# Expert layer on one core: the weight split behind the last activation, a drain replaced by a count, weight sums spread over seven experts

## The chip, the cores and the metric

The kernel runs on one core of one Trainium2 chip. The metric is the device time of one execution, in microseconds; lower is better. Engine names in the profile: PE is TensorE (PEld its weight loads), DVE is VectorE, ACT is ScalarE, POOL is GpSimd, SP is SyncE, which only issues DMAs here.

## What is computed

Four residual layers over 4096 tokens of width 256: a linear-memory attention, a mixture of experts, an RWKV time and channel mix, and a gated network with ternary weights. The change lies in the mixture of experts, and in the preparation of sums of the last layer's hidden weights, which runs beside it. The mixture, as the reference has it (top 2 of 8 experts, hidden size 1024):

```
logits = xf @ w_router
probs = softmax(logits); topk_w, topk_idx = top_k(probs, 2)
h = gelu(einsum('te,ieh->tih', xf, w1) + b1)
out = einsum('tih,ihe->tie', h, w2) + b2
out = sum(out * weights[..., None], axis=1)
```

## The kernel before

**Tiles.** The stage before has sorted the tokens by expert, as rows `z1_by_expert` in memory. A tile is 256 rows of one expert; there are 35 tiles here, four or five per expert, and their number per expert is read at run time. Each engine runs `expert_tiles`: for every expert one call of its `step` for the first tile, and a loop of `step` for the others. In the first tile `before` is the expert before, in the others it is the expert itself; the test `before < e` so marks an expert's first tile.

**Products.** Every matrix product is made of three, from a high and a low part of each operand (`mm3`, lines 1468 to 1470). The parts: high = a copy rounded to the short form, low = raw minus high. For weights, ScalarE makes the high part (`high_part`, line 1654) and VectorE the low part (`low_part`, line 1740), each 128 x 2048 elements; both matrices of an expert have two buffers, used in turn. For the hidden activations `h`, VectorE makes both parts, two blocks of 128 at a time (lines 1757 and 1759).

**One tile on TensorE** (`step` of `pe`): `up(e, t)`, 8 blocks m of 6 matmuls, into four banks used in turn; from block 4 on a block waits until ScalarE has taken the one four blocks before (`h_act`, the GELU of line 1665). Then `rows_T(t + 1)`, four transposes of the next tile's rows, and `down(before, t)`, 48 matmuls on the h of the tile before. `hs_free` tells VectorE after each quarter of `down` that a pair of h has been read. After `down` in an expert's first tile TensorE drains and increments `ex_done` (line 1629).

**One tile on ScalarE**: in a first tile, if there is a next expert (`ahead`: experts 0 to 6), wait until its weights have landed and make the high part of its w1; 8 GELUs; in a first tile wait for `ex_done` and make the high part of w2; then `gated(t)` (line 1651): wait for both halves of `yt` and for the landing of the scatter before (`y_out`), and scale by the gates into `yg`.

**One tile on VectorE**: gates; in a first tile the low part of the next w1; `rows_split(t + 1)` (the next tile's rows, lines 1713 to 1717); four pairs of h, of which the fourth comes behind `y(before, t)`, the bias sums `yt` (line 1725), one for each of the two banks of `down`; the rows' token numbers (line 1730), `hand_on` (line 1735); in a first tile the low part of the next w2.

**One tile on POOL**: two scatters with addition of `yg` to the token rows (line 1542, `y_out`). In the first tile of experts 1 to 6 `hidden_sums` is called behind it (lines 1547 to 1561): DMAs that add one 512 x 512 block of a hidden weight matrix in memory to another, in halves of 512 KB, all in POOL's queue like the scatters. Experts 1 and 2 have four of them, 3 to 6 two. In expert 7 two multiplications for the next stage's weights follow (line 1534). SyncE loads the rows of tiles ahead, and the raw weights of expert e + 2, two buffers in turn.

Of the kernel before, what the change touches and what calls it, by code (L numbers as in the profile page):

```python
# [28 lines left out]
NP7 = 7  # L29
# [47 lines left out]
def build(nc, A):  # L77
# [5 lines left out]
    with ctx:  # L83
# [1369 lines left out]

        ew_rdy, ex_done = sem2("w1_split"), sem2("expert_done")
        eb_ld, xg_ld, xt_ps, xT_rdy = (sem2("expert_biases_loaded"), sem2("rows_loaded"), sem2("rows_T_in_psum"),
# [70 lines left out]
        def _(pool):  # L1526
# [17 lines left out]

            def add_blocks(to, source):
                for k in (0, 2):
                    pool.dma_start(hw_rows[to][:, k:k + 2, :], source[:, k:k + 2, :], accum_op=ALU.add).then_inc(hw_add, 16)

            def hidden_sums(n):

                layer, base = n % 2, n % 2 * NP7
                if n < 2:
                    pool.wait_ge(hw_cp, 16 * 2 * NP7)
                    for i in (W_S3, W_S1):
                        add_blocks(base + i, quarter(layer, 1, 0))
                elif n < 4:
                    pool.wait_ge(hw_add, 16 * 8)
                    add_blocks(base + W_S2, hw_rows[base + W_S1])
                elif n < 6:
                    pool.wait_ge(hw_add, 16 * 12)  # L1560
                    add_blocks(base + W_S4, hw_rows[base + W_S2])

# [18 lines left out]
        def _(pe):  # L1581
            T = nc.tensor
            pe.sem_inc(xt_ps, 1)
            pe.sem_inc(ex_done, 2)

# [36 lines left out]
            def step(e, t, before, start):  # L1622

                up(e, t)
                rows_T(t + 1)
                if not start:
                    down(before, t)
                    if before < e:
                        pe.drain().then_inc(ex_done, 1)

# [6 lines left out]
        def _(act):  # L1637
# [18 lines left out]
            def step(e, t, before, start):  # L1656
                ahead = before < e and e + 1 < NE
                if ahead:
                    act.wait_ge(*landed(e + 1))
                    high_part(w1s, raw1, e + 1)  # L1660
                for m in range(KH):
                    act.wait_ge(up_ps, t * KH + (m + 1))
                    if m % 2 == 0:
                        act.wait_ge(h_rdy, t * 4 + (m // 2 + 1))
                    nc.scalar.activation(h32[:, m, :], B[m % 4][:, 0:TT], ACT.Gelu_apprx_tanh,  # L1665
                                         bias=b1s[:, e * KH + m:e * KH + m + 1]).then_inc(h_act, 1)
                    if start and m == 5:
                        act.wait_ge(ew_rdy, 1)
                        act.wait_ge(w2_rdy, 1)
                        act.dma_start(st1[:, :, :], w1_d[2]).then_inc(nw_ld[0], 16)  # L1670
                        act.dma_start(st2[:, :, :], w2_d[2]).then_inc(nw_ld[0], 16)
                if ahead:
                    act.wait_ge(ex_done, e + 2)
                    high_part(w2s, raw2, e + 1)
                if not start:
                    gated(t)
# [10 lines left out]
        def _(dve):  # L1687
# [54 lines left out]
            def step(e, t, before, start):  # L1742
                ahead = before < e and e + 1 < NE
                gate_of(e, t)
                if ahead:
                    low_part(w1s, raw1, e + 1, 2 * e + 3, ew_rdy)
                rows_split(t + 1)
                for m in range(0, KH, 2):
                    i = m // 2
                    dve.wait_ge(h_act, t * KH + (m + 2 + 4))  # L1750
                    if i < 3:
                        dve.wait_ge(hs_free, t * 3 + (i + 1))
                    else:
                        if not start:
                            y(before, t)
                        dve.wait_ge(dn_ps, t * 2 + 2)
# [1678 lines left out]
```

## Time and profile before

| | us |
|---|---|
| three timed runs | 2024.34, 2028.38, 2029.12 |
| their median | 2028.38 |
| the profiled execution | 2018.43 |
| its span | 2016.4 |
| expert stage in it (first transposes to last product) | about 522 to 962 |
| TensorE busy over the span | 1829.2 (91%) |
| VectorE busy | 1488.2 (74%) |
| ScalarE busy | 1114.2 (55%) |
| GpSimd busy | 316.7 (16%) |

Busy time is how long an engine executed; the rest is idle. In a timeline a bracket behind an instruction gives how long its engine had been idle before it and whose work ended that. Matmuls are pipelined: each is drawn 0.28 us long while the next begins 0.11 us after it.

### The profile page before, as it was taken

The page shows a single profiled execution, that of the slowest core. Times are in us where ns is not written, and L with a number is a line of the kernel's source. Part 1 is how long each engine was busy: PE and PEld are TensorE (multiplying, and loading weights), DVE is VectorE, ACT ScalarE, POOL GpSimd, SP SyncE. Part 2 cuts the span into 40 slices and gives each one's busy share as a digit, 9 for nine tenths or more (in the row PEclk, how much of TensorE's full clock was granted, in tenths as well). Part 3 has the DMA queues.
Part 4 walks back from the last instruction along what each step waited for, and adds up shares of the span by engine and source line. Part 5 has one row for each costly group of instructions (what it writes and reads, how often), then busy time and mean ns, then how long its engine had stood idle before and what let it go on. Part 6 is the DMA issues. An engine that isn't in the chain of part 4 may idle for free. (4 is left out here: it accounts for less than half of the span.)

```text
span 2016.4 us, 31206 instructions
## 1 busy us (share of the span) xinstructions
PE 1829.2 (91%) x10840; PEld 1561.6 (77%) x10840; DVE 1488.2 (74%) x2966; ACT 1114.2 (55%) x1987; POOL 316.7 (16%) x282
## 2 busy tenths in 40 slices
PE   8999999996598899999577758999999999999999
PEld 5688888885598899999455536677788888888887
DVE  7567888787566666666599879999686776776675
ACT  4656666663444344343688857665456456456454
POOL 0000012234344233333100011111000000000000
PEclk9999999995799999999788879999999999999999
DMA  3199434413456545442444553333333143143141
GB/s 110 50 389 402 127 123 143 146 65 121 121 115 141 116 89 109 70 64 38 125 112 88 111 100 132 150 124 123 122 142 146 34 176 146 41 177 117 53 177 64
DMA packets 107986, 251.79 MB, mean 125 GB/s; under 512 B 8992, under 2 KB 51616, under 8 KB 99616
## 3 DMA queue, kind: packets, MB, share of 16 engines
q1 hardware_dynamic: 82288, 201.16, 28.2%
q0 software_dynamic: 23680, 46.28, 12.4%
q10 hardware_dynamic: 1888, 2.67, 0.4%
q8 instruction: 75, 1.23, 0.3%
q14 instruction: 55, 0.45, 0.1%
HBM read 172.88 MB, written 107.61 MB: 139 GB/s over the span
## 5 line engine op out<-in xcount | busy, mean ns | idle before, releaser
L1542 POOL DMA_INDIRECT tokens_behind_spare_rows<-yg,row_of_token x70 | 128.9, 1841 | 295.6 <-DVE row_of_token L1730 265.3
L1665 ACT ACTIVATE h<-bank,b1s 128x256 f32<-128x256 f32 x280 | 124.0, 471 | 33.5 <-PE bank L1470 21.1
L3172 ACT ACTIVATE hidden_quarter<-hidden_quarter,scl 128x512 f32<-128x512 f32 x96 | 67.6, 721 | 118.9 <-DVE hidden_quarter L3008 117.8
L1651 ACT ACTIVATE yg<-yt,own_gates 128x256 f32<-128x256 f32 x68 | 30.8, 501 | 183.3 <-DVE yt L1725 162.2
L1223 PE MATMUL bank<-st,L 128*128 128x128 f32 x768 | 117.4, 279 | 13.3 <-DVE st L573 13.2
L957 ACT ACTIVATE L<-bank 128x512 f32<-128x512 f32 x128 | 75.1, 593 | 94.7 <-PE bank L1215 94.4
L2381 PE MATMUL bank<-split_0h,hidden_weights 128*128 128x512 f32 x320 | 126.5, 395 | 0.0
L2381 PE MATMUL bank<-split_1h,hidden_weights 128*128 128x512 f32 x320 | 125.4, 392 | 0.1
L2382 PE MATMUL bank<-split_0l,hidden_weights 128*128 128x512 f32 x320 | 125.3, 391 | 0.0
L2382 PE MATMUL bank<-split_1l,hidden_weights 128*128 128x512 f32 x320 | 125.3, 391 | 0.0
L1215 PE MATMUL bank<-L 128*128 128x128 f32 x640 | 119.4, 277 | 0.0
L1223 PEld LDWEIGHTS bank<-st,L 128*128 128x128 f32 x768 | 100.6, 193 | 17.8 <-DVE st L573 7.0
L573 DVE TENSOR_TENSOR st<-st,bank 128x256 f32<-128x256 f32 x192 | 75.1, 417 | 52.9 <-PE bank L1223 52.1
L1214 PE MATMUL bank<-L 128*128 128x128 f32 x512 | 101.4, 280 | 0.7
L2381 PE MATMUL bank<-split_2h,hidden_weights 128*128 128x512 f32 x256 | 101.4, 396 | 0.0
L1759 DVE TENSOR_TENSOR hsl<-h,hsh 128x512 fp32r<-128x512 f32 x140 | 96.9, 692 | 4.8
L2382 PE MATMUL bank<-split_2l,hidden_weights 128*128 128x512 f32 x256 | 100.2, 391 | 0.0
L1215 PEld LDWEIGHTS bank<-L 128*128 128x128 f32 x640 | 95.5, 194 | 0.0
L1468 PE MATMUL bank<-xTh,w_1h 128*128 128x256 f32 x288 | 80.8, 281 | 11.0 <-ACT h L1665 8.9
L1468 PE MATMUL bank<-xTh,w_0h 128*128 128x256 f32 x272 | 78.3, 288 | 12.7 <-ACT h L1665 9.5
L2960 DVE SCALAR_TENSOR_TENSOR hidden_quarter<-bank,scl,x_tok 128x512 f32<-128x512 f32 x64 | 47.4, 748 | 55.6 <-ACT x_tok L3135 55.6
L2967 DVE TENSOR_TENSOR split_2l<-hidden_quarter,split_2h 128x1024 fp32r<-128x1024 f32 x48 | 59.1, 1253 | 35.4 <-ACT split_2h L3154 35.4
(485 smaller groups left out, 6020.2 us busy)
## 6 DMA issues: line engine op xcount, KB each, us to landing
hidden_weights<-hidden_weight_blocks SPq DMA_DIRECT2D x64, 1024.0 KB, 4.9
z_by_expert<-zero SPq DMA_DIRECT2D x64, 520.0 KB, 15.7
hidden_weight_blocks<-in_ffn_dram SPq DMA_DIRECT2D x14, 1024.0 KB, 9.8
ckb<-in_ffn_dram POOLq DMA_DIRECT2D x32, 352.0 KB, 5.5
xg<-z_by_expert SPq DMA_DIRECT2D x36, 260.0 KB, 3.3
x_tok<-in_w_dram SPq DMA_DIRECT2D x8, 1024.0 KB, 10.1
x_tok<-x_T SPq DMA_DIRECT2D x16, 512.0 KB, 6.3
x_tok<-after_time_mix SPq DMA_DIRECT2D x15, 512.0 KB, 8.5
```

Of the source, the lines that this page charges most:

```text
L573: V.tensor_tensor(z_ if SQUARES <= n < LEVELS - 1 else x_, x_, B[2 + j][:, 0:256], ALU.subtract if n == 0 else ALU.add).then_inc(ap_rdy, 1)
L957: A_.activation(L[:, p, j, (n + 1) % 2, :, :], src, ACT.Copy).then_inc(sq_cp, 1)
L1214: T.matmul(B[j][:, 256 * m:256 * m + 128], b_, a, start=True, stop=True)
L1215: last = T.matmul(B[j][:, 256 * m + 128:256 * m + 256], a, b_, start=True, stop=True)
L1223: last = T.matmul(B[2 + j][:, 0:256].rearrange("p (a m d) -> p a m d", a=2, m=2)[:, :, m, :], Ln[:, 2 * m + 1, :], right, start=True, stop ...
L1468: nc.tensor.matmul(out, a[0], b[0], start=first, stop=False)
L1542: pool.indirect_dma_start(x2_d, bass.IndirectOffsetOnAxis(to_row[:, j:j + 1].bitcast(u32), 0), yg[:, j, :], None, compute_op=ALU.add).then ...
L1665: nc.scalar.activation(h32[:, m, :], B[m % 4][:, 0:TT], ACT.Gelu_apprx_tanh, bias=b1s[:, e * KH + m:e * KH + m + 1]).then_inc(h_act, 1)
L1759: V.tensor_tensor(hs[1][:, m:m + 2, :], h32[:, m:m + 2, :], f32(hs[0][:, m:m + 2, :]), ALU.subtract).then_inc(h_rdy, 1)
L2381: nc.tensor.matmul(out, w, x[0], start=first, stop=False, **more)
L2382: return nc.tensor.matmul(out, w, x[1], start=False, stop=last, **more)
L3172: A_.activation(QB[to][:, m, :], src, ACT.Gelu, scale=scl[:, off[lay.name] + row:off[lay.name] + row + 1]).then_inc(g_act, 1)
```

## The change

Three edits. ScalarE's high part of the next w1 moves from ahead of the eight GELUs to behind them, and VectorE's low part of it from ahead of the row split to ahead of `y`, behind the third pair of h. The drain of TensorE and its semaphore `ex_done` go; ScalarE waits for `dn_ps`, which the last matmuls of `down` increment and which VectorE's `y` waits for already. The 16 adding DMAs are issued at experts 1 to 7 as 2, 2, 2, 2, 2, 3, 3, in place of 4, 4, 2, 2, 2, 2, with the waits for the sums that they read.

```diff
--- before.py
+++ after.py
@@ -1451,7 +1451,7 @@
             second_sems.append(ptwo.enter_context(nc.semaphore(name)))
             return second_sems[-1]
 
-        ew_rdy, ex_done = sem2("w1_split"), sem2("expert_done")
+        ew_rdy = sem2("w1_split")
         eb_ld, xg_ld, xt_ps, xT_rdy = (sem2("expert_biases_loaded"), sem2("rows_loaded"), sem2("rows_T_in_psum"),
                                        sem2("rows_T_split"))
         up_ps, h_act, h_rdy, dn_ps, y_rdy, y_out = (sem2("up_in_psum"), sem2("gelu_done"), sem2("h_split"),
@@ -1542,23 +1542,30 @@
                     pool.indirect_dma_start(x2_d, bass.IndirectOffsetOnAxis(to_row[:, j:j + 1].bitcast(u32), 0), yg[:, j, :], None,
                                             compute_op=ALU.add).then_inc(y_out, 16)
 
-            def add_blocks(to, source):
-                for k in (0, 2):
-                    pool.dma_start(hw_rows[to][:, k:k + 2, :], source[:, k:k + 2, :], accum_op=ALU.add).then_inc(hw_add, 16)
-
             def hidden_sums(n):
 
-                layer, base = n % 2, n % 2 * NP7
-                if n < 2:
+                def add(layer, to, half, more=None):
+                    base = layer * NP7
+                    source = quarter(layer, 1, 0) if more is None else hw_rows[base + more]
+                    k = 2 * half
+                    pool.dma_start(hw_rows[base + to][:, k:k + 2, :], source[:, k:k + 2, :], accum_op=ALU.add).then_inc(hw_add, 16)
+
+                if n == 0:
                     pool.wait_ge(hw_cp, 16 * 2 * NP7)
-                    for i in (W_S3, W_S1):
-                        add_blocks(base + i, quarter(layer, 1, 0))
-                elif n < 4:
-                    pool.wait_ge(hw_add, 16 * 8)
-                    add_blocks(base + W_S2, hw_rows[base + W_S1])
-                elif n < 6:
-                    pool.wait_ge(hw_add, 16 * 12)
-                    add_blocks(base + W_S4, hw_rows[base + W_S2])
+                for half in range(2):
+                    if n < 4:
+                        add(n % 2, (W_S3, W_S1)[n // 2], half)
+                    elif n < 6:
+                        pool.wait_ge(hw_add, 16 * 8)
+                        add(n % 2, W_S2, half, W_S1)
+                if n == 5:
+                    pool.wait_ge(hw_add, 16 * 10)
+                    add(0, W_S4, 0, W_S2)
+                if n == 6:
+                    pool.wait_ge(hw_add, 16 * 13)
+                    add(0, W_S4, 1, W_S2)
+                    for half in range(2):
+                        add(1, W_S4, half, W_S2)
 
             def step(e, t, before, start):
                 add_to_tokens(t)
@@ -1581,7 +1588,6 @@
         def _(pe):
             T = nc.tensor
             pe.sem_inc(xt_ps, 1)
-            pe.sem_inc(ex_done, 2)
 
             def rows_T(n):
 
@@ -1625,8 +1631,6 @@
                 rows_T(t + 1)
                 if not start:
                     down(before, t)
-                    if before < e:
-                        pe.drain().then_inc(ex_done, 1)
 
             pe.sem_inc(hs_free, 3)
             rows_T(0)
@@ -1655,9 +1659,6 @@
 
             def step(e, t, before, start):
                 ahead = before < e and e + 1 < NE
-                if ahead:
-                    act.wait_ge(*landed(e + 1))
-                    high_part(w1s, raw1, e + 1)
                 for m in range(KH):
                     act.wait_ge(up_ps, t * KH + (m + 1))
                     if m % 2 == 0:
@@ -1670,7 +1671,9 @@
                         act.dma_start(st1[:, :, :], w1_d[2]).then_inc(nw_ld[0], 16)
                         act.dma_start(st2[:, :, :], w2_d[2]).then_inc(nw_ld[0], 16)
                 if ahead:
-                    act.wait_ge(ex_done, e + 2)
+                    act.wait_ge(*landed(e + 1))
+                    high_part(w1s, raw1, e + 1)
+                    act.wait_ge(dn_ps, t * 2 + 2)
                     high_part(w2s, raw2, e + 1)
                 if not start:
                     gated(t)
@@ -1742,8 +1745,6 @@
             def step(e, t, before, start):
                 ahead = before < e and e + 1 < NE
                 gate_of(e, t)
-                if ahead:
-                    low_part(w1s, raw1, e + 1, 2 * e + 3, ew_rdy)
                 rows_split(t + 1)
                 for m in range(0, KH, 2):
                     i = m // 2
@@ -1751,6 +1752,8 @@
                     if i < 3:
                         dve.wait_ge(hs_free, t * 3 + (i + 1))
                     else:
+                        if ahead:
+                            low_part(w1s, raw1, e + 1, 2 * e + 3, ew_rdy)
                         if not start:
                             y(before, t)
                         dve.wait_ge(dn_ps, t * 2 + 2)
```

## Rows read from the trace of the kernel before

**Rows 1.** the page: busy time of TensorE, its granted clock in 40 slices

```profile
PE 1829.2 (91%) x10840; PEld 1561.6 (77%) x10840; DVE 1488.2 (74%) x2966; ACT 1114.2 (55%) x1987; POOL 316.7 (16%) x282
...
PEclk9999999995799999999788879999999999999999
```

**Rows 2.** the windows: us, busy us of each engine, PEclk, DMA share, GB/s

```profile
750.00:810.00 60.00, 58.00 (x500) 57.61 (x499) 40.19 (x92) 25.60 (x52) 20.49 (x12) 1.00 0.48 97
```

**Rows 3.** the waits of TensorE, 500 to 975: total us, times, longest

```profile
PE bank L1468 <- ACT h L1665: 18.4, 10, 3.7
```

**Rows 4.** the timeline: start, length, what, idle before; first tile, expert 3

```profile
681.26 0.39 PE L1468 MATMUL bank<-xTh,w_1h 128*128 128x256 f32 x1 [1.45 <-ACT h L1665]
```

**Rows 5.** timelines at the end of that tile; groups L1740 and L1629

```profile
689.46 0.69 DVE L1759 TENSOR_TENSOR hsl<-h,hsh 128x512 fp32r<-128x512 f32 x1
690.07 0.77 DVE L1725 TENSOR_TENSOR yt<-bank,b2s 128x256 f32<-128x256 f32 x2
...
L1740 DVE TENSOR_TENSOR w_1l<-x_tok,w_1h x8: 2283/2288/2293, 527.3 to 874.3; 128x2048 fp32r<-128x2048 f32 x8
...
690.46 1.92 ACT L1654 ACTIVATE w_0h<-st 128x2048 fp32r<-128x2048 f32 x1 [5.66 <-PEq L1629]
692.28 0.89 ACT L1651 ACTIVATE yg<-yt,own_gates 128x256 f32<-128x256 f32 x2
693.08 2.71 ACT L1665 ACTIVATE h<-bank,b1s 128x256 f32<-128x256 f32 x6
...
690.89 0.38 PE L1468 MATMUL bank<-xTh,w_1h 128*128 128x256 f32 x1 [0.52 <-issue]
...
L1629 PEldq DRAIN  x7: 2307/2307/2308, 581.4 to 916.0; - x7
```

**Rows 6.** timelines around the sums; DMA issues with landing; windows of the clock

```profile
591.74 5.46 POOL L1547 DMA_DIRECT2D hidden_weight_blocks<-in_ffn_dram  x4
698.46 2.37 POOL L1547 DMA_DIRECT2D hidden_weight_blocks<-hidden_weight_blocks  x2
707.12 1.55 POOL L1542 DMA_INDIRECT tokens_behind_spare_rows<-yg,row_of_token  x1 [0.30 <-issue]
...
tokens_behind_spare_rows<-yg,row_of_token POOLq DMA_INDIRECT x1, 4.1
...
st<-in_w_dram SPq DMA_DIRECT2D x1, 1024.0 KB, 10.2
...
612.59 0.91 ACT L1651 ACTIVATE yg<-yt,own_gates 128x256 f32<-128x256 f32 x2 [10.65 <-DMA tokens_behind_spare_rows<-yg,row_of_token]
...
613.90 0.39 PE L1468 MATMUL bank<-xTh,w_1h 128*128 128x256 f32 x1 [3.66 <-ACT h L1665]
...
666.39 0.38 PE L1468 MATMUL bank<-xTh,w_0h 128*128 128x256 f32 x1 [3.48 <-ACT h L1665]
...
612.00:619.00 7.00, 5.09 (x44) 5.10 (x45) 2.35 (x9) 4.25 (x10) 3.09 (x2) 1.00 1.01 316
...
666.00:672.00 6.00, 5.61 (x35) 5.61 (x36) 1.27 (x7) 3.32 (x8) 3.07 (x2) 0.72 0.63 126
```

**Rows 7.** timelines of expert 7

```profile
908.58 2.09 ACT L1665 ACTIVATE h<-bank,b1s 128x256 f32<-128x256 f32 x5 [0.51 <-DVE hsl L1759]
...
923.61 4.23 POOL L1534 TENSOR_TENSOR x_tok<-x_tok 128x768 f32<-128x768 f32 x2
...
925.20 2.68 DVE L1713 COPY raw_gates<-xg 128x8 f32<-128x8 f32 x1 [4.46 <-PE bank L1591]
...
934.49 0.38 PE L1468 MATMUL bank<-xTh,w_1h 128*128 128x256 f32 x1 [0.94 <-ACT h L1665]
```

**Rows 8.** the timeline of SyncE in the channel-mix stage

```profile
1206.07 1.71 SPq L2439 DMA_DIRECT2D hidden_weights<-hidden_weight_blocks  x3
```

**Rows 9.** timelines of expert 0, second tile

```profile
535.27 0.38 PE L1468 MATMUL bank<-xTh,w_0h 128*128 128x256 f32 x1 [1.66 <-ACT h L1665]
...
536.85 1.40 ACT L1665 ACTIVATE h<-bank,b1s 128x256 f32<-128x256 f32 x3
```


## The prediction

> **What bounds the kernel now.** I read the page first: TensorE is busy 91% of the span, and its clock is at its higher level nearly throughout [rows 1]. Then the stretches of the expert stage, about 520 to 962 us, where all the edits lie: in its steady part TensorE is busy 58 of 60 us, VectorE 40, ScalarE 26 [rows 2]. So only idle time of TensorE can be won there. The list of who waited for whom says what it idles for: ten times for a GELU of ScalarE, 18.4 us in total, the longest 3.7 us [rows 3]. The timelines at an expert's change show where these are.
>
> A tile is 48 matmuls up and 48 down, 0.116 us each start to start (58.0 us by 500 [rows 2]). The up half needs GELU 0 of its own tile before its 25th matmul, 2.8 us after its first. A gap of TensorE listed as idle g costs g + 0.17, since a matmul is drawn 0.28 us long but follows the last after 0.11.
>
> Three kinds of gaps. **First**, in the first tile of experts 1 to 6 ScalarE does the high part of the next w1 (1.92 us) ahead of the GELUs, and TensorE idles 1.45 us [rows 4] (the 1.92 is a row of [rows 5]): loss 1.62, six times: six of the ten waits of [rows 3] are of this kind. **Second**, behind the down half of that tile TensorE drains, and its next up half starts 0.52 us idle later: loss 0.69, seven times [rows 5]. **Third**, in the third tile of experts 1 and 2 ScalarE waits 10.65 us for the scatter of the tile before (it overwrites `yg`), and TensorE idles 3.66 and 3.48 us: loss 3.83 and 3.65. Behind the second the clock is 0.72 of full over 6 us: 0.28 x 6 = 1.7 us more; behind the first it stays at 1.00 [rows 6].
>
> **The change part by part**, on the profiled execution, 2018.43 us with a span of 2016.4.
>
> **(a) High and low part of w1 moved, experts 1 to 6.** The 1.62 of the first kind goes: expert 7, which has no high part, shows its GELUs right behind the gating and no gap [rows 7]. ScalarE then does the high part after GELU 7, in about 5 us in which it waited for the drain (5.66 idle [rows 5]), so that costs nothing. The low part is not so lucky. VectorE has to do it (2.29 us [rows 5]) between the third pair of h and the bias sums `y`. In the timeline the third pair's subtraction starts at 689.46 and ends about 690.15, and `yt` follows at once at 690.07: VectorE has no hole there. So `yt` comes 2.2 us later, at 692.28, done at 693.05; the gating copies of ScalarE wait for both halves of it, run from 693.16, and GELU 0 of the next tile, queued behind them, runs from 693.98 to 694.45 (the spacing 692.28, 693.08 of now). The high part of w2, released by the down products at 690.4, is done at 692.4 and is hidden behind that wait.
>
> **(b) Drain removed.** TensorE's next up half starts at 690.21 in place of 690.89. Its 25th matmul is due 0.68 earlier too, at 692.93, and meets GELU 0 at 694.48: a new loss of 1.55. So for each of experts 1 to 6: -1.62 - 0.69 + 1.55 = -0.76, in all **-4.6**. Even without (a) the drain's gain would mostly be given back: GELU 0 is now ready at 693.55 [rows 5], 0.62 after that earlier due time. Expert 7 has no weights to split, there the whole **-0.7** counts.
>
> **(c) Sums spread.** Now four accumulating transfers are issued in each of the first two places, two in each of four more; after it is two in five places and three in the last two. With four, the second scatter of the next tile lands when it releases ScalarE, at 612.6, that is 20.8 after the first transfer's issue at 591.74; with two it lands 4.1 after 707.12, at 711.2, 12.8 after 698.46 [rows 6]. Without loss ScalarE may get it up to about 17.0 (612.6 - 3.8 - 591.7). So in experts 1 and 2 the wait goes whole: -3.83 - 3.65 - 1.7 = **-9.2**. The bound on the other side: weights of 1 MB from SyncE take 10.2 us in the same stretch [rows 6], and would have to delay the scatter by more than 4 us to bring it back.
> By the Trainium skill (DMA: Bandwidth & Descriptors, Anatomy of one DMA) such a transfer takes 2.0 us plus its bytes over 436 GB/s, 3.2 us for 512 KB. By that four in a row with the two scatters behind them would be through in some 14 us and would delay nobody, and term (c) would be nothing. The rows show 20.8 and the wait; they decide.
>
> Three transfers (experts 6 and 7): between 12.8 and 20.8, at the mean 16.8 against 17.0. No stall, or up to 0.7 each; I take **+0.3**. Nobody is late for the sums: SyncE first reads the blocks at 1206 [rows 8], 260 us behind the last.
>
> **(d) Expert 0.** Here the moved work was free: both parts of w1 of expert 1 ran before or beside the first tile, where everybody waited. After, the high part (1.92) lies ahead of tile 1's GELUs, now at 536.85: GELU 0 ends 539.1 against a 25th matmul due 2.87 after 535.27, 538.1: loss 1.0. The low part delays the splitting of h by 2.2; `yt` of tile 1, by my count of VectorE's queue, comes some 1.1 behind the down products, which costs 0.5 in tile 2. **+1.5**; bounds 1.0 and 2.6 (nothing of the 2.2 absorbed beyond what TensorE already lost) [rows 9].
>
> **(e) Expert 7's products.** POOL's two multiplications for the time-mix weights take 4.23 us from 923.61; VectorE's copy of 128x8 elements, due at 925.20, took 2.68, until they were over, and TensorE lost 0.94 + 0.17 = 1.1 in the next tile [rows 7]. After, three transfers stand ahead of them. Two occupy POOL 2.37, four 5.46 [rows 6], three about 3.5. The products then start near 927, in VectorE's busy part, not with their first 1.6 us in its hole. **+1.6**, between 0 (they interleave as now) and 3.3 (with the clock's 1.7 on a gap that grows to 2.7).
> The Trainium skill (SBUF — State Buffer, two separate sides) says that the port pair of VectorE and GpSimd is an exclusive lock held for a whole instruction by whichever starts first. By that the whole 4.2 us count against VectorE, which gives the same 1.6; the copy's 2.68 agrees. If it did not hold at the new place, the term would be 0.
>
> Sum: -4.6 - 0.7 - 9.2 + 0.3 + 1.5 + 1.6 = **-11.1 us**, 2007.3 on the profiled execution. The median of the three timed runs is 2028.38, 10 above the profiled one and with a spread of 4.8; none of the terms hangs on that, so 2028.4 - 11.1 = **2017.3**.
>
> **The rivals.**
> **R1, the low part is hidden.** If VectorE found room for it (pairs of h taken earlier), the 1.55 would not come, nor expert 0's 0.5: 2017.3 - 9.8 = 2007.5. For it: VectorE is busy for 40 of 60 us only. Against: its holes are not in that place, where `yt` follows the third pair at once [rows 5], and program order puts the low part straight ahead of `yt`.
> **R2, the wait for the scatter stays.** Weight loads or the now later scatters keep ScalarE waiting in experts 1 and 2, or the threes stall as the fours did: up to 9.2 comes back, 2026.5. For it: the two expert changes with the long waits are also those with weight loads. Against: with two transfers no place of four shows a wait.
> **R3, slower: the clock.** Six new gaps of 1.55 us and one or two in experts 0 and 7 come behind another tile's end. If each made the clock fall to its lower level (1.2 of 2.4 GHz) for 6 us, as wide as the window of [rows 6], each would cost 3 us: 7 x 3 = 21, 2038. It decides from 11.1/7 = 1.6 us a place, a fall of 3.2 us. Against: six gaps of 1.45 and one of 3.66 left it at 1.00 [rows 2, 6].
> **R4, the change does nothing that shows**: gains in one place turn up as waits in another, (a) and (b) at zero, (d) and (e) at their upper ends: 2028.4 - 9.2 + 2.6 + 3.3 + 1.4 = 2026.5, like R2.
>
> **How the numbers follow.** Forecast 0.60, R1 0.10, R2 and R4 0.20, R3 0.10. Within the forecast the bounds of (c), (d) and (e) reach from 2015 to 2021, and the median of another set of runs moves by some 3 us either way, as the three here do. The range from R1's edge to R2's: 2009 to 2026. About 0.3% (6 us) is what a measurement tells from no change. Faster by more than that (under 2022.3): the forecast and R1, with a part of each lost to the runs' scatter, and some of R2: 0.72. Within: most of R2 and R4 and a tail of the forecast, 0.21. Slower: 0.07, most of R3.
>
> **What the profile would show.** Right: no gap of TensorE in first tiles; a gap of about 1.4 idle in the second tile of experts 1 to 6, with ScalarE's gating waiting for `yt`, and `yt` directly behind the low part; no wait of `yg` on the scatter in experts 1 and 2; no low clock near 666; a gap over 2 us in expert 7. Wrong: no gap in second tiles (R1), `yg` waiting for DMA (R2), a low clock behind the new gaps (R3). The sum would be wrong if the profiled execution's 10 us under the median stood for gaps that I do not see.

## The result, and the profile after

The changed kernel takes 2017.99 us (median of six runs, 2011.9 to 2019.4), the kernel before 2029.06 on the same chip. The ratio is 0.9941, with a 95% interval of 0.9930 to 0.9951: 11 us, or 0.6%, faster. On another chip the same pair gave 0.9947 (0.9933 to 0.9962). The forecast was 2017.3, 11.1 us faster.

The profiled execution after took 2017.27 us. Its page answers to [rows 1]:

```profile
span 2015.1 us, 31198 instructions
PE 1829.8 (91%) x10840; PEld 1563.2 (78%) x10840; DVE 1489.5 (74%) x2966; ACT 1114.9 (55%) x1987; POOL 307.6 (15%) x282
PEclk9999999996699999999788889999999999999999
```

Its span is only 1.3 us below the 2016.4 of the trace before. That looks like no gain at all; why it is one, and where the 11 us are, is told below with the kernel before run again. First the views of the expert stage. The waits of TensorE, which answer to [rows 3] (columns: total us, times, longest):

```profile
PE bank L1468 <- ACT h L1666: 11.8, 8, 3.2
```

Eight waits for a GELU are left of ten, 11.8 us of 18.4. Six of them are one new gap. The timelines of VectorE, ScalarE and TensorE at the end of expert 3's first tile, which answer to [rows 5]:

```profile
687.53 2.29 DVE L1743 TENSOR_TENSOR w_0l<-st,w_0h 128x2048 fp32r<-128x2048 f32 x1
689.73 0.75 DVE L1728 TENSOR_TENSOR yt<-bank,b2s 128x256 f32<-128x256 f32 x2
...
687.87 1.93 ACT L1658 ACTIVATE w_0h<-st 128x2048 fp32r<-128x2048 f32 x1 [3.81 <-PE bank L1470]
690.60 0.91 ACT L1655 ACTIVATE yg<-yt,own_gates 128x256 f32<-128x256 f32 x2 [0.80 <-DVE yt L1728]
691.41 1.55 ACT L1666 ACTIVATE h<-bank,b1s 128x256 f32<-128x256 f32 x4
...
691.92 0.39 PE L1468 MATMUL bank<-xTh,w_1h 128*128 128x256 f32 x1 [1.35 <-ACT h L1666]
```

The low part of w1 runs from 687.53, right where `yt` stood before; `yt` follows at 689.73, 2.2 us later. ScalarE has the high part of w2 done at 689.80 and idles 0.80 us for `yt`, gates, and its GELU at 691.41 releases TensorE's 25th matmul at 691.92, after 1.35 us idle, a loss of 1.51. The gap ahead of it in the first tile [rows 4] and the one behind the drain are gone.

The second place is expert 7, where POOL, VectorE, ScalarE and TensorE answer to [rows 7]; the last line is a window with its clock (columns as in [rows 2]):

```profile
919.94 3.18 POOL L1551 DMA_DIRECT2D hidden_weight_blocks<-hidden_weight_blocks  x3
921.63 5.18 POOL L1534 TENSOR_TENSOR x_tok<-x_tok 128x768 f32<-128x768 f32 x2
...
920.55 0.87 DVE L1716 COPY raw_gates<-xg 128x8 f32<-128x8 f32 x1 [3.48 <-PE bank L1597]
...
922.65 4.45 DVE L1760 CAST hsh<-h 128x512 fp32r<-128x512 f32 x1
...
930.74 0.91 ACT L1655 ACTIVATE yg<-yt,own_gates 128x256 f32<-128x256 f32 x2 [10.15 <-DVE yt L1728]
...
932.06 0.58 PE L1468 MATMUL bank<-xTh,w_1h 128*128 128x256 f32 x1 [3.16 <-ACT h L1666]
...
931.00:938.00 7.00, 5.94 (x28) 5.94 (x29) 1.45 (x6) 3.94 (x10) 3.21 (x2) 0.51 0.91 155
```

The three sums are issued first, and beside them VectorE's copy of 128x8 elements takes 0.87 us in place of 0.17. POOL's products reach into VectorE's busy part, and the copy of the first pair of h, 128x512, takes 4.45 us in place of 0.42. `yt` and the gating come late, TensorE idles 3.16 us, and for the 7 us behind that its clock is 0.51 of full.

The third is the scatter. The waits of ScalarE in the stage:

```profile
ACT yg L1655 <- DVE yt L1728: 177.2, 33, 10.1
ACT yg L1655 <- DMA tokens_behind_spare_rows<-yg,row_of_token: 6.8, 1, 6.8
```

Before, `yg` waited for the DMA twice, 21.1 us in total, one of them the 10.65 of [rows 6]; now it waits once, in expert 6, for 6.8 us. In other tiles it waits 6.2 us there for `yt` anyway, and TensorE shows no gap.

### The profile page after: what moved, and what is told of

Read it like the earlier page. It is cut to its first block and busy times, and to the rows that moved or that the text cites. A ratio compares the mean times of both kernels' runs of the same rounds, so it can differ in the third digit from the quotient of the medians.

```text
span 2015.1 us, 31198 instructions
## 1 busy us (share of the span) xinstructions
PE 1829.8 (91%) x10840; PEld 1563.2 (78%) x10840; DVE 1489.5 (74%) x2966; ACT 1114.9 (55%) x1987; POOL 307.6 (15%) x282
## 3 DMA queue, kind: packets, MB, share of 16 engines
q8 instruction: 75, 1.23, 0.3%
## 5 line engine op out<-in xcount | busy, mean ns | idle before, releaser
L1542 POOL DMA_INDIRECT tokens_behind_spare_rows<-yg,row_of_token x70 | 119.2, 1702 | 298.7 <-DVE row_of_token L1733 277.0
L1666 ACT ACTIVATE h<-bank,b1s 128x256 f32<-128x256 f32 x280 | 123.7, 472 | 36.3 <-PE bank L1470 21.1
L1223 PE MATMUL bank<-st,L 128*128 128x128 f32 x768 | 117.2, 279 | 13.3 <-DVE st L573 13.2
```

Of the source, the lines that this page charges most:

```text
L1223: last = T.matmul(B[2 + j][:, 0:256].rearrange("p (a m d) -> p a m d", a=2, m=2)[:, :, m, :], Ln[:, 2 * m + 1, :], right, start=True, stop ...
L1542: pool.indirect_dma_start(x2_d, bass.IndirectOffsetOnAxis(to_row[:, j:j + 1].bitcast(u32), 0), yg[:, j, :], None, compute_op=ALU.add).then ...
```

## The experiments

Each ratio is of runs against runs of the kernel before on the same chip. "Stage" is what I read from each trace beside it: from the start of the experts' first up product to the start of their last down product. It leaves out what happens ahead of the stage, which differs between executions.

| kernel | median us | before, same chip | ratio (95%) | stage in its trace |
|---|---|---|---|---|
| before, first trace | | | | 436.7 |
| before again | 2027.95 | 2027.18 | 1.0002 (0.9990 to 1.0013) | 439.5 |
| changed | 2017.99 | 2029.06 | 0.9941 (0.9930 to 0.9951) | 429.1 |
| changed again | 2015.91 | 2027.18 | 0.9947 (0.9933 to 0.9962) | 426.3 |
| sums only | 2013.10 | 2018.97 | 0.9964 (0.9951 to 0.9977) | 431.4 |
| sums only, again | 2023.62 | 2031.38 | 0.9962 (0.9951 to 0.9973) | 430.5 |
| w1's parts only | 2017.83 | 2018.97 | 0.9989 (0.9973 to 1.0004) | 435.8 |
| drain only | 2023.10 | 2018.97 | 1.0014 (1.0000 to 1.0028) | 436.4 |
| changed, low part behind yt | 2002.62 | 2018.97 | 0.9915 (0.9894 to 0.9936) | 422.0 |
| the same again | 2015.01 | 2031.38 | 0.9917 (0.9901 to 0.9933) | 421.2 |
| changed, products first | 2013.20 | 2027.18 | 0.9937 (0.9921 to 0.9952) | 424.2 |
| changed, drain back | 2019.27 | 2031.38 | 0.9939 (0.9924 to 0.9955) | 428.4 |
| all three repairs | 2007.80 | 2027.18 | 0.9909 (0.9893 to 0.9925) | 418.9 |
| repairs and POOL's order | 2011.72 | 2031.38 | 0.9901 (0.9884 to 0.9918) | 420.3 |

### The kernel before and the changed kernel, once more

No edit in either.

> The kernel before against itself: ratio 1 within its interval. Its trace tells whether the low clock comes behind one or both waits for the scatter (one in the first trace: 3.4 us of low clock, 1.7 us of loss each).

> The changed kernel once more, against the kernel before on the same chip as the next three. Theory: of the 11 us measured first, the expert stage's own traces hold 7.7 (from its first up product to its last product); the rest is the runs' scatter and the low clock that comes or stays away behind a gap. Expected 7 to 11 us faster. Rival (something outside the stage got faster too): 11 us or more again, and the trace shows it behind the last product of the experts.

The kernel before gave 1.0002 against itself, and a span of 2028.7 us, 12.3 more than its first trace. The difference lies ahead of the experts' products. ScalarE begins the stage by clearing 67 semaphores (line 1640) before it makes expert 0's high parts. The group of these clears (duration in ns as min/median/max, then start of first and last) and the first high part behind them, first trace:

```profile
L1640 ACTq EVENT_SEMAPHORE_RANGE_CLEAR  x67: 41/41/46, 505.2 to 509.5; - x67
...
509.63 3.71 ACT L1643 ACTIVATE w_0h<-st 128x2048 fp32r<-128x2048 f32 x2 [9.99 <-issue]
```

and again, with the first up product of TensorE:

```profile
L1640 ACTq EVENT_SEMAPHORE_RANGE_CLEAR  x67: 1/41/710, 512.1 to 528.4; - x67
...
528.51 1.91 ACT L1643 ACTIVATE w_0h<-st 128x2048 fp32r<-128x2048 f32 x1 [21.68 <-issue]
...
534.37 0.57 PE L1468 MATMUL bank<-xTh,w_0h 128*128 128x256 f32 x1 [3.20 <-DVE xTl L1717]
```

In the one they run from 505.2 to 509.5, in the other from 512.1 to 528.4, single ones up to 0.7 us. The first up product comes 9.6 us later (534.37, against 524.82 in the first trace); with the 2.8 by which the stage itself was longer that makes the 12.3. Of the 9.6, 6.9 were there before the clears began; where they arise I did not follow. The changed kernel's trace is of the second kind (511.1 to 526.7), the kernel before's first trace of the first kind; its first up product comes 7.8 us later (532.66), and so the two spans differ by 1.3 us only. By the stage alone they differ by 436.7 - 429.1 = 7.6, and the two later ones, both of the second kind, by 439.5 - 426.3 = 13.2. The changed kernel timed 10.7 us below on that chip (0.9947), inside the 7 to 11 expected. The rival there, a gain behind the experts, is out: from the end of the last down product to the end of the span it is 1054.6 us in both traces of before, 1053.1 and 1055.4 in those of the changed kernel.

Why 13.2 and not 7.6: in the kernel before again, ScalarE's waits for the scatter, and two windows with the clock (a window's line ends with TensorE's clock, the DMAs' share and GB/s):

```profile
ACT yg L1651 <- DMA tokens_behind_spare_rows<-yg,row_of_token: 22.1, 2, 11.6
...
620.00:632.00 12.00, 7.37 (x51) 7.28 (x51) 2.99 (x10) 4.26 (x10) 3.09 (x2) 0.86 0.84 255
676.00:686.00 10.00, 7.31 (x49) 7.31 (x50) 2.88 (x10) 4.26 (x10) 3.07 (x2) 0.83 0.66 174
```

The clock fell behind both waits, 0.86 over 12 us and 0.83 over 10: 1.7 us of loss each, where the first trace had it behind the second wait alone. The one wait was longer, too (TensorE lost 4.8 at it, not 3.8). The changed kernel's two traces differ as well: behind the gap in expert 7 the low clock lasted 6.8 us in the first and 3.4 in the second, and the stage began at the low clock for 6.0 us in the first and 2.9 in the second (5.4 and 4.9 in those of before).

### The sums alone

```diff
-                if n < 2:
+                if n == 0:
...
-                    for i in (W_S3, W_S1):
-                        add_blocks(base + i, quarter(layer, 1, 0))
+                    if n < 4:
+                        add(n % 2, (W_S3, W_S1)[n // 2], half)
```

(the whole third edit of the change, and none of the others)

> The kernel before with the spread sums alone; w1's parts and the drain stay where they were. Theory: the two waits for the scatter in experts 1 and 2 go (3.83 + 3.65 us) and with them the low clock behind the second (1.7 us), 9.2 in all; in expert 7 three transfers stand ahead of POOL's products, which costs there 2.2 us of gap and, as in the changed kernel's trace, up to 3.4 us of low clock behind it. So 3.6 to 7.0 us faster than before. Rival R2 (the waits for the scatter come back with the weight loads): 0 to 2 us slower, and the trace shows yg waiting for the DMA in third tiles. Rival (most of the measured 11 us comes from the sums): 9 us or more faster.

> The kernel before with the spread sums alone, once more, beside the others of this call. Expected as the first run had it: 5 to 8 us faster than before; rival: on a chip where the low clock comes behind both waits for the scatter, 2 us more.

Measured: 7.3 us faster, and again 7.7 (0.9962 of 2031.38). The first is 0.3 above the band of the first expectation, the second inside its own. TensorE's waits for GELUs, and VectorE's small copy in expert 7:

```profile
PE bank L1468 <- ACT h L1672: 10.8, 7, 2.2
...
915.49 5.50 DVE L1720 COPY raw_gates<-xg 128x8 f32<-128x8 f32 x1 [4.27 <-PE bank L1598]
```

Both long waits are gone. The copy of 128x8 elements, 2.68 us in [rows 7], takes 5.50: three transfers and then the products stand in POOL. It ends with the products, which are drawn from 915.78 to 920.96. The load of the next rows, issued at 921.22 behind the sums, took 10.6 us where the median of the trace is 3.3, and TensorE idled 1.28 us for it. So this kernel holds the change's part (c) and its cost (e) together. The stage is 5.3 us shorter than the first one of before, and in the second pair of traces, where before lost 1.7 more to the clock and 1.0 more to the wait, 9.0. R2 is out: no wait for the scatter came back with the weights' loads.

### w1's parts alone

```diff
-                if ahead:
-                    act.wait_ge(*landed(e + 1))
-                    high_part(w1s, raw1, e + 1)
                 for m in range(KH):
...
                 if ahead:
+                    act.wait_ge(*landed(e + 1))
+                    high_part(w1s, raw1, e + 1)
                     act.wait_ge(ex_done, e + 2)
...
-                if ahead:
-                    low_part(w1s, raw1, e + 1, 2 * e + 3, ew_rdy)
                 rows_split(t + 1)
...
+                        if ahead:
+                            low_part(w1s, raw1, e + 1, 2 * e + 3, ew_rdy)
                         if not start:
                             y(before, t)
```

> The kernel before with the two parts of the next w1 moved, and nothing else: the drain, its semaphore and the sums as before. Theory: 1.62 us are won in the first tile of experts 1 to 6; the low part delays yt by 2.2, GELU 0 of the second tile is ready at about 694.5 on the timeline of expert 3 against a due time of 693.7 behind the drain, a loss of 0.8; net -0.8 six times, +1.4 in expert 0: 3.5 us faster. Rival R1 (the low part is hidden): 9.7 - 1.0 = 8.7 us faster and no gap in second tiles. Rival (the high part's place never mattered): no change.

Measured 2.2 us faster, between 5.4 faster and 0.8 slower, so no change is not excluded by the times. The trace is clearer. TensorE's waits (GELUs, and those behind the drain, called issue):

```profile
PE bank L1468 <- ACT h L1662: 13.8, 10, 4.3
PE bank L1468 <- issue: 3.7, 7, 0.5
```

The six gaps of 1.6 are gone from the first tiles, and in six second tiles there is one of 0.7 (the 0.8 expected) behind the drain's 0.7. Expert 0 lost 1.67. The two scatter waits grew a little (3.71 and 4.46 lost), and the clock fell behind both. R1, the low part hidden, would have been 8.7 us and is refuted.

### The drain alone, and the change with the drain put back

```diff
-                    if before < e:
-                        pe.drain().then_inc(ex_done, 1)
...
-                    act.wait_ge(ex_done, e + 2)
+                    act.wait_ge(dn_ps, t * 2 + 2)
                     high_part(w2s, raw2, e + 1)
```

(and the reverse of it on the changed kernel)

> The kernel before with the drain replaced by the count of down products, nothing else. Theory: TensorE starts the next up half 0.68 us earlier but meets GELU 0 at its 25th matmul 0.62 later than that earlier due time, because ScalarE's high part of w2 takes 1.92 us from the same moment as before: net -0.07 six times and -0.7 in expert 7, so 1.1 us faster, not to be told from no change, and a gap of about 0.45 us idle in second tiles in place of the one behind the drain. Rival (the drain costs what it shows): 0.69 x 7 = 4.8 us faster and no gap in second tiles.

> The changed kernel with the drain and its semaphore back, the other two parts as changed. Theory: yt, late by the low part, sets GELU 0 of the second tile anyway, so experts 1 to 6 lose nothing by the drain (it hides under the 1.5 us gap) and only expert 7 loses 0.7: 0 to 1.5 us slower than the changed kernel, 10 to 11 faster than before. Rival (each drain costs its 0.7): 4.8 us slower than the changed kernel, 6 to 7 faster than before.

The drain alone: ratio 1.0014, from no change to 0.3% slower; a gain of 4.8 us is excluded. ScalarE and TensorE at expert 3's second tile:

```profile
688.50 1.93 ACT L1651 ACTIVATE w_0h<-st 128x2048 fp32r<-128x2048 f32 x1 [5.62 <-PE bank L1470]
690.33 0.89 ACT L1648 ACTIVATE yg<-yt,own_gates 128x256 f32<-128x256 f32 x2
691.12 1.18 ACT L1662 ACTIVATE h<-bank,b1s 128x256 f32<-128x256 f32 x3
...
691.63 0.38 PE L1468 MATMUL bank<-xTh,w_1h 128*128 128x256 f32 x1 [0.44 <-ACT h L1662]
```

The drain's 0.52 idle of [rows 5] has become 0.44 idle at the 25th matmul, because the high part of w2, 1.93 us from the moment that the down products end, sets GELU 0. The changed kernel with the drain back is as fast as without (0.9939 beside 0.9941 and 0.9947), 12.4 us faster than before where 10 to 11 were expected; the rival's 6 to 7 lies outside its interval (9.1 to 15.4). Its timeline of TensorE shows how the 1.5 us splits in two:

```profile
689.90 0.38 PE L1468 MATMUL bank<-xTh,w_1h 128*128 128x256 f32 x1 [0.52 <-issue]
693.46 0.39 PE L1468 MATMUL bank<-xTh,w_1h 128*128 128x256 f32 x1 [0.55 <-ACT h L1669]
```

0.52 behind the drain and 0.55 at the 25th matmul: losses of 0.69 and 0.72, together 1.41 against 1.51. So a wait removed ahead of a later one that it hid under is worth nothing.

In expert 7 the drain's 0.69 was not won either. VectorE and TensorE there, in the drain-only trace:

```profile
922.11 3.67 DVE L1710 COPY raw_gates<-xg 128x8 f32<-128x8 f32 x1 [3.48 <-PE bank L1590]
...
932.39 0.38 PE L1468 MATMUL bank<-xTh,w_1h 128*128 128x256 f32 x1 [1.93 <-ACT h L1662]
```

Without the drain the small copy comes 0.6 us behind the start of POOL's products, not 1.6. It is held for 3.67 us in place of 2.68, and TensorE loses 2.10 in place of 1.11: 1.0 more, against the 0.69 gained. That is 0.3 us; that the drain alone came out 2.8 us slower than before by its times, with a stage 0.3 shorter, stays unexplained.

### The low part of w1 behind yt

```diff
-                        if ahead:
-                            low_part(w1s, raw1, e + 1, 2 * e + 3, ew_rdy)
                         if not start:
                             y(before, t)
+                        if ahead:
+                            low_part(w1s, raw1, e + 1, 2 * e + 3, ew_rdy)
```

> The changed kernel with one pair of lines swapped: VectorE makes the low part of w1 behind yt and ahead of the fourth pair of h, not ahead of yt. Theory (yt late by the low part is what opens the 1.5 us gap in second tiles): yt comes with the down products again, and ScalarE's high part of w2 sets GELU 0: a gap of about 0.6 us in place of 1.5, so 0.9 us less six times; VectorE then has both low parts ahead of the next row split, 1.2 us more than its hole there, which may give back up to 0.7 each. 1 to 6 us faster than the changed kernel, 12 to 17 faster than before. Rival (VectorE's load as a whole, not the order, sets the gap): the gap moves one tile on and the time stays at 11 us faster than before.

> The changed kernel with the low part of w1 behind yt, once more, on the chip of this call: the first run stood beside other kernels on another chip. Theory: the second tiles' gap is 0.6 in place of 1.5, the clock behind expert 7's gap stays low, so 5.5 us less than the changed kernel: 16 to 17 us faster than before.

Measured 0.9915 and 0.9917, 17.2 and 16.9 us faster than before. VectorE, ScalarE and TensorE at the same tile:

```profile
676.64 0.69 DVE L1762 TENSOR_TENSOR hsl<-h,hsh 128x512 fp32r<-128x512 f32 x1
677.25 0.77 DVE L1728 TENSOR_TENSOR yt<-bank,b2s 128x256 f32<-128x256 f32 x2
677.93 2.29 DVE L1743 TENSOR_TENSOR w_0l<-st,w_0h 128x2048 fp32r<-128x2048 f32 x1
...
677.59 1.93 ACT L1658 ACTIVATE w_0h<-st 128x2048 fp32r<-128x2048 f32 x1 [3.81 <-PE bank L1470]
679.42 0.89 ACT L1655 ACTIVATE yg<-yt,own_gates 128x256 f32<-128x256 f32 x2
...
680.72 0.39 PE L1468 MATMUL bank<-xTh,w_1h 128*128 128x256 f32 x1 [0.44 <-ACT h L1666]
```

`yt` follows the third pair again, the low part comes behind it, ScalarE goes from the high part of w2 to the gating without a pause, and TensorE idles 0.44 in place of 1.35. Six times 0.91 is 5.5 us, and the two traces' stages are on average (421.6) 4.7 below that of the changed kernel's second trace and 7.5 below the first. No gap opened a tile later in experts 1 to 6: VectorE did the two low parts and the small steps before the next rows came. So the order cost 0.9 of the 1.5 us a place, and VectorE's load nothing; the other 0.6 is what the high part of w2 costs once the drain is gone.

### POOL's products ahead of the last sums

```diff
-                if before < e and e >= 1:
-                    hidden_sums(e - 1)
                 if before < e and e == NE - 1:
                     time_mix_weights()
+                if before < e and e >= 1:
+                    hidden_sums(e - 1)
```

> The changed kernel with POOL's two products ahead of the last sums in expert 7, as they stood before. Theory (three transfers ahead of the products push them into VectorE's busy part): the gap in expert 7 goes back from 3.3 us of loss to 1.1 and the low clock behind it (6.8 us, 3 us of loss) goes: 5 us faster than the changed kernel, 13 to 16 faster than before. Rival (the three sums themselves, by their descriptors, hold VectorE up): the gap stays above 2 us, the time within 2 us of the changed kernel's.

Measured 0.9937, 12.8 us faster than before; beside the changed kernel's 0.9947 on the same chip 2 us, not 5, with intervals that overlap. That is just under the 13 to 16 expected. The stage is 2.1 shorter.

```profile
914.89 4.23 POOL L1534 TENSOR_TENSOR x_tok<-x_tok 128x768 f32<-128x768 f32 x2
919.41 2.61 POOL L1551 DMA_DIRECT2D hidden_weight_blocks<-hidden_weight_blocks  x3 [0.30 <-POOL x_tok L1534]
...
915.49 3.66 DVE L1716 COPY raw_gates<-xg 128x8 f32<-128x8 f32 x1 [3.48 <-PE bank L1597]
...
925.76 0.38 PE L1468 MATMUL bank<-xTh,w_1h 128*128 128x256 f32 x1 [1.92 <-ACT h L1666]
...
936.88 0.91 ACT L1655 ACTIVATE yg<-yt,own_gates 128x256 f32<-128x256 f32 x2 [7.61 <-DMA tokens_behind_spare_rows<-yg,row_of_token]
```

POOL's products and sums, VectorE's copy, TensorE's gap and ScalarE's next gating, in this order. The low clock is gone, as expected. But the gap is 1.92 idle, not 0.94: the copy is held up 3.66 us, not 2.68, as in the drain-only kernel (3.67), since without the drain the next rows are there 1.0 us earlier against the products, which still start behind the scatters. The rival, that the sums hold it, is out for this copy: it ends at 919.15, and the first sum is issued at 919.41. And the sums, now issued 4.5 us later, keep the next scatter: `yg` waits 7.61 us for the DMA and TensorE loses 0.79. The theory had one price for this place; it holds two, and they trade against each other.

### All three repairs, and POOL's queue in another order

The first is the two edits above, and for expert 0 both parts of w1 where they were before:

```diff
+                if ahead and start:
+                    act.wait_ge(*landed(e + 1))
+                    high_part(w1s, raw1, e + 1)
                 for m in range(KH):
...
                 gate_of(e, t)
+                if ahead and start:
+                    low_part(w1s, raw1, e + 1, 2 * e + 3, ew_rdy)
                 rows_split(t + 1)
```

> The changed kernel with three repairs: the low part of w1 behind yt, the products ahead of the last sums, and in expert 0 both parts of w1 where they were before. Theory: the terms add: against the changed kernel -0.9 x 6 - 5.2 - 1.4 = -12.0, so 20 to 23 us faster than before. Rival (the gaps trade places once more): no more than 17, as with the low part's place alone.

The second has these repairs of w1's parts, and POOL's step in another order (`between` runs behind the wait for `to_rdy`, ahead of the scatters):

```diff
-                add_to_tokens(t)
-                if before < e and e == NE - 1:
-                    time_mix_weights()
                 if before < e and e >= 1:
                     hidden_sums(e - 1)
+                add_to_tokens(t, time_mix_weights if before < e and e == NE - 1 else None)
```

> The three repairs together (low part of w1 behind yt, expert 0 as before) and POOL's queue in another order: the sums are issued ahead of the wait for the tile's scatter, when POOL sits idle, and the products of expert 7 between that wait and the two scatters, in VectorE's hole of 3 to 4.5 us before the next rows arrive. Theory (a gap in expert 7 comes from VectorE being held up, and from the scatter queued behind the sums): no gap over 0.5 us in expert 7 and no wait of yg for a DMA; the 3 us which the three repairs still lose there go, 22 to 24 us faster than before. Rival (POOL's products slow VectorE wherever they stand): the gap of 2 stays, 19 us.

Measured 18.4 us faster than before (0.9909) and 20.1 (0.9901). Both are faster than the change, and their intervals overlap with each other and with the low part's place alone (0.9917): the repairs do not add to the 20 to 23 expected of the first, and the second falls short of its 22 to 24. In the second, three lines show TensorE's transposes in expert 7, ScalarE's one wait for the scatter (in expert 3), and all that is left of waits for GELUs:

```profile
916.68 0.66 PE L1597 MATMUL bank<-ident,xg 128*128 128x128 f32 x4 [2.73 <-DMA xg<-z_by_expert]
...
ACT yg L1655 <- DMA tokens_behind_spare_rows<-yg,row_of_token: 6.5, 1, 6.5
...
PE bank L1468 <- ACT h L1669: 2.6, 6, 0.4
```

The products now hold up two of VectorE's small operations only (1.23 and 1.70 us), in its hole, and six waits for GELUs of 0.4 are all that remain. The scatter comes 0.3 us later than `yt` would have let `yg` go, which costs TensorE nothing. But the sums, issued from 902.17 to 903.32, now lie ahead of or beside the load of the next rows, issued at 903.29: it takes 13.3 us, where the median of the trace is 3.6, and the transposes wait 2.73 us for it. So its theory missed: the gap moved from the third tile to the second.

## Why the prediction was right, point by point

The losses of TensorE in the stage (idle + 0.17 for each gap, half of the time that it ran at the lower clock), step by step:

| step | forecast | first traces | second traces |
|---|---|---|---|
| (a), (b) experts 1 to 7 | -5.3 | -5.5 | -5.4 |
| (c) waits of experts 1 and 2 | -7.5 | -7.5 | -8.4 |
| (c) clock behind them | -1.7 | -1.7 | -3.3 |
| (c) three transfers, expert 6 | +0.3 | 0.0 | 0.0 |
| (d) expert 0 | +1.5 | +1.4 | +0.8 |
| (e) expert 7, gap | +1.6 | +2.2 | +2.0 |
| (e) clock behind it | 0 | +3.0 | +1.7 |
| clock at the stage's start, no term of the forecast | | +0.3 | -1.0 |
| sum | -11.1 | -7.8 | -13.6 |
| stage, as measured | | -7.6 | -13.2 |

**(a) and (b)** came as worked out in experts 1 to 6: the new loss was 1.51 in each (forecast 1.55), by the chain named: low part, `yt`, gating, GELU 0. The low part swapped with `yt` shows that the order causes 0.9 of it, and the two drain kernels that the drain's gain is given back. In expert 7 the whole 0.7 was counted as won; the drain-only trace shows it given back there as well, and more, as part of (e).

**(c)** was right in its mechanism and too small in one term. The lower clock follows such a wait in most cases, not in one of two: in the four traces of kernels that still had four transfers in experts 1 and 2 it came behind seven of the eight waits (2.0 to 4.8 us lost at each). I had taken the one trace's one of two. The rule that I weighed, of the Trainium skill (DMA: Bandwidth & Descriptors, Anatomy of one DMA: 2.0 us and bytes over 436 GB/s), would have made (c) nothing; the sums alone gave 7.3 and 7.7 us. For adding transfers from memory to memory in POOL's queue its figure does not hold here: of the four in expert 1 of the first trace the first landed 8.8 us after its issue, and the last 17.1 us after that issue, with the two scatters behind it.

**The three transfers**: the second scatter landed 16.9 and 16.1 us after their first issue in expert 6, against an estimate of 16.8 and an edge of 17.0: no loss, and 0.79 in expert 7 when they were issued 4.5 us later there (17.4). The mean of the values for two and four was luck as a way to it: with two, the scatter is issued only 8.7 us after the first transfer and lands 4.1 later, where a scatter with nothing ahead of it mostly takes 3.7 to 3.9, so that 12.8 says little of the queue.

**(d)** was 1.42 in the first trace, but not where it was forecast: TensorE waited for rows at the transposes (0.69) and for GELU 0 in tile 2 (0.73), and at GELU 0 of tile 1, where the 1.0 was forecast, not at all. The wait for rows is no work of the change: the kernel before, run again with the long clears, has it too (0.75). The second trace shows both forecast places, 0.85 in tile 1 and 0.70 in tile 2. With the 0.75 of before off, 0.8 is new.

**(e)** is the term that was mis-sized: 1.6 forecast, 5.2 and 3.7 measured. The mechanism held: VectorE's operations are held until POOL's products are over. But I let only 1.6 us more of that count. The copies were held for 2.51 us before (2.68 against 0.17), and for 4.73 after: 4.03 in the copy of h, and 0.70 in the small copy, which ran while POOL only issued the sums. That is 2.2 more, and the gap's loss grew by 2.2, to 3.3 and not 2.7. The lower clock behind it, which I had put at the upper end of the bounds, came in both traces of the changed kernel. And the sums in front are only 1.2 of the 2.2: with the drain gone and no transfer ahead of the products TensorE lost 2.10 (drain alone) and 2.09 (products first), against 1.11 before. The other 1.0 comes from removing the drain, a path that the prediction did not have.

All but 1.4 us of what holds VectorE in this place reaches TensorE: held 2.51, 2.71, 3.49 and 4.73 us (before, before again, products first, changed), lost 1.11, 1.30, 2.09 and 3.33. As to the rule of the Trainium skill that I weighed (SBUF — State Buffer, two separate sides: an exclusive lock for a whole instruction), the copies of 2.68, 3.66 and 5.50 us agree with it, each ending within 0.05 us of the end of POOL's second product; the one of 4.45 ends 0.3 behind it. Each was held through the end of the first product as well. The small copy's 0.87 shows a holdup without a product; that the issuing of the sums makes it is likely, not shown.

So the 11.1 came out right with luck. In the first pair of traces (e) is 3.6 worse than forecast and little makes up for it: the stage is 7.6 shorter. In the second, (c) is 2.5 better and (e) 2.1 worse, (d) and the clock at the stage's start help by 1.7, and it is 13.2 shorter. The times, 11.1 and 10.7 us, lie between the two. **The median**: that none of the terms hangs on the 10 us between the profiled execution and the timed ones held as far as the traces tell. The second trace of before took 2030.74, and 9.6 of the 12.3 us between the two spans lay ahead of the stage; of the timed executions there is no trace.

**The rivals.** R1 did not come (the gaps are there). The order-swapped kernel shows that 5.5 us of its 9.8 could be had; the price was too high, since without the low part the high part of w2 still sets GELU 0, 0.6 behind its due time. R2 did not come. R3, the clock falling at each new gap: it fell behind none of the 1.5 us gaps in two traces, but did behind the one of 3.3. Its price was too high as well: 3 us a place were taken for the whole window of [rows 6], which itself shows 1.7. R4: the gains did not turn up as waits elsewhere, but for (e).

What stays open: by their times w1's parts and the drain alone give 2.2 us faster and 2.8 slower, and with the 7.3 of the sums 6.7 in all, against 11 measured for the three. The intervals (each some 3 us either way) hold the difference; the stages of the traces (0.9, 0.3 and 5.3) sum to 6.5 of 7.6 in the first pair.

## What to carry to other kernels

Before an item moves to where its engine is idle, look at what stands right behind it in program order on that engine, and who waits for that: the low part cost 0.9 us a place ahead of `yt` and nothing that shows behind it. A wait or a drain counts only beyond the next wait on the same chain. Work that starts earlier can meet another engine's work: without the drain VectorE ran longer into POOL's products. And two traces of one kernel can differ by more than the change is worth; compare them by the stretch that the change touches.

## What the runs showed of the hardware

- The clearing of 67 semaphores by ScalarE took 4.3 us in five traces and 16 in nine, single clears up to 0.73 us. All four traces of one chip were of the short kind, and that chip timed the kernel before at 2019 us against 2027 to 2031 on the others; what makes it stays open.
- TensorE's clock fell from 2.4 to 1.2 GHz for 3.4 us, in one place 6.8, beginning between 0.9 us before and 1.4 us behind a gap's end. It did so at seven of eight scatter waits (2.0 to 4.8 us lost at each) and at every gap of 2.9 to 3.3 in expert 7 (five traces), and never behind a lone gap of 1.5 to 1.7. All these are losses, idle + 0.17. Near 2 us it went both ways: it fell once at 2.0, three times it did not at 2.1, and behind a 2.3 that had a 1.5 close ahead of it, it fell in two traces of three.
- Adding transfers of 512 KB in POOL's queue: with four ahead of it the second scatter behind them landed 19.0 to 21.8 us after their first issue, with three in expert 6 15.8 to 16.9, and with two 11.6 to 14.5 (all issued behind a tile's scatters). A load of 260 KB of rows from SyncE, issued behind or with the third of three, took 10.6 to 13.7 us in three traces (median 3.3 to 3.6), and TensorE idled 0, 1.3 and 2.7 us for it.
- A 128x512 copy of VectorE, 0.42 us by itself, took 4.45 while POOL multiplied 128x768 tiles. A 128x8 copy, 0.17 by itself, took 2.68 to 5.54 beside them, and 0.87 while POOL only issued adding transfers.
